# An eight-core Hyena and mixture-of-experts layer: the routing weights taken by eight compares and sums per token group instead of two maximum trees

## The chip, the cores and the metric

The kernel runs on all 8 cores of one Trainium2 chip, the same program on each, with no exchange between them. The time is device time in microseconds of the slowest core. Engines are named as in the profile: PE (TensorE), DVE (VectorE), ACT (ScalarE), POOL (GpSimd), SP (SyncE).

## The reference, cut to what matters

Input x is 4 sequences of 8192 tokens of width 1024. The layer has two halves, each with a layer norm before and behind it: a long convolution, and a mixture of 8 experts with the two best taken for each token. Only the second half is touched by the change, and in it only the weights `combine`:

```python
normed = _rmsnorm(x, norm_weight)
logits = jnp.einsum('bsd,ed->bse', normed, router_weight)      # 8 experts
probs = jax.nn.softmax(logits, axis=-1)
topk_w, topk_idx = jax.lax.top_k(probs, 2)
topk_w = topk_w / jnp.sum(topk_w, axis=-1, keepdims=True)
combine = jnp.sum(jax.nn.one_hot(topk_idx, E) * topk_w[..., None], axis=-2)
for e in range(8):
    gate, up = halves of einsum('bsd,hd->bsh', normed, gate_up_weight[e])   # 2816 each
    out_e = einsum('bsh,dh->bsd', silu(gate) * up, down_weight[e])
    moe_out = moe_out + combine[..., e, None] * out_e
```

## The kernel before

Each core takes 4096 tokens. Three stages come first, to about 1,410 us of the span: constants and the filter, input projection with short convolution, and long convolution with output projection and norms. The last one leaves `s_x1`, `s_xn2` and `s_normed` in HBM. The fourth stage, D, is the mixture, and holds all that the change touches.

Stage D runs over 4 token blocks `tb` of 1024 tokens, and in each over 8 experts `e_`. All experts are computed for all tokens. For one expert, 11 sections of weights (`guw`, two buffers, loaded by POOL's queue) are gone through; each section has four passes (two halves of the tokens by two chunks of 128 hidden columns), each of them 8 matmuls into `pg` (L1010; three PSUM buffers), 8 into `pup` (L1019; two buffers), one Silu on ACT from `pg` to `sil` (L1030) and one product on DVE, `hid` = `sil` times `pup` (L1035). PE may write a `pup` buffer again only when the product that read it is done (`pup_last`). After the sections come four quarters of the down projection (L1068, weights `dnw`), each with 8 token groups of 22 matmuls into `pd`, and DVE adds every result into `acc`, weighted by one column of `comb` (L1079 for expert 0, L1082 for the others).

The weights `comb` of block tb come from two functions. `routing_prep(tb)` loads the transposed activations `nrm` by SP's queue, lets PE compute the router logits (64 matmuls of 8 columns into `plog`, L863), and has DVE copy all 64 columns of `plog` to `cLL` (L872). `dance_tg(tb, tg)` then works on one group of 128 tokens, 8 logits each: a tree of three maxima gives the largest (L890 to L894), it is negated (L896), ACT takes the exponential of the logits (L898), the largest is masked out (L899 to L903), a second tree gives the second largest (L905 to L909), ACT takes the exponential of their difference (L913), and DVE builds the denominator, the mask of the two winners, the masked exponentials, the reciprocal and their product (L915 to L927). These are 17 DVE instructions and 2 on ACT, nearly each behind a semaphore wait on the one before; with the copy, 137 DVE instructions for one block.

Where they stand in the queues: block 0's routing comes before the first expert. Block tb+1's comes right behind expert 0's down projection of block tb, so ahead, in the order of DVE and ACT, of every Silu and every product of expert 1. For tb = 1 to 3 each expert is also followed by `e_chunk(tb - 1, e_)`, which finishes 128 tokens of the block before (L949 to L959, with a layer norm over `ffnE`). With 4 blocks there are 4 routings, and `e_chunk` stands behind the third and the fourth.

Of the kernel before, what the change touches and what calls it, by code (L numbers as in the profile page):

```python
# [7 lines left out]
F32 = mybir.dt.float32  # L8
BF16 = mybir.dt.bfloat16
AF = mybir.ActivationFunctionType  # L10
ALU = mybir.AluOpType
AX = mybir.AxisListType
# [169 lines left out]
def build_nc(debug=False, phases=("0", "AB", "C", "D"), ab_stage=5, nb=NB,  # L182
             ntb=NTB, nexp=NEXP, d_stage=4):
    nc = bass.Bass("TRN2", target_bir_lowering=False)
# [37 lines left out]
    k = K(nc)  # L222

    chb = Ch(nc, "bar")
    ch_v = Ch(nc, "v")
    ch_a = Ch(nc, "a")
    ch_p = Ch(nc, "p")
    ch_pe = Ch(nc, "pe")
# [64 lines left out]
    m1 = k.op("tensor", lambda e: e.matmul(p_h1[:, :], t_w2[:, :], t_s1[:, :], start=True, stop=True), ch_pe)  # L293
# [502 lines left out]
    if "D" in phases:  # L796
        esD = ExitStack()
# [6 lines left out]
                for p in range(2)]  # L804
        combB = [esD.enter_context(nc.sbuf_tensor(f"comb{p}", [128, (TB // 128) * 8], F32))
                 for p in range(2)]
        cLL = esD.enter_context(nc.sbuf_tensor("cLL", [128, 64], F32))
        cR = esD.enter_context(nc.sbuf_tensor("cR", [128, 8], F32))
        cE = esD.enter_context(nc.sbuf_tensor("cE", [128, 8], F32))
        cS = esD.enter_context(nc.sbuf_tensor("cS", [128, 8], F32))  # L810
        cM = esD.enter_context(nc.sbuf_tensor("cM", [128, 8], F32))
        smD = esD.enter_context(nc.sbuf_tensor("smD", [128, 16], F32))
        sil = [esD.enter_context(nc.sbuf_tensor(f"sil{i}", [128, 512], F32)) for i in range(3)]
        x1r = [esD.enter_context(nc.sbuf_tensor(f"x1r{i}", [128, 1024], BF16)) for i in range(2)]
# [9 lines left out]
        plog = esD.enter_context(nc.psum_tensor("plog", [128, 64], F32))  # L824

        NTG = TB // 128
# [6 lines left out]
        sil_last = {0: 0, 1: 0, 2: 0}  # L833
        plog_read = 0
        dance_a_prev = 0
        dance_p_prev = 0
        dance_v_prev = 0
        comb_done = {}
        uv_end = {}
        dcp_mark = {}  # L840

        ntrv = [0, 0]
        gu_end = {}

        def routing_prep(tb):
            nonlocal plog_read
            p = tb % 2
            t0p = tb * TB
            k.wait("sync", ch_pe, gu_end.get(tb - 2, 0))
            for tkb in range(2):  # L850
                for dc in range(DCN):
                    k.dma("sync", nrmB[p][tkb][:, dc * 512:(dc + 1) * 512],
                          bass.AP(s_normed, (t0p + tkb * 512) * D + dc * 128, [[D, 512], [1, 128]]),
                          ch_ntrP[p], transpose=True)
            ntrv[p] = ch_ntrP[p].n
            k.wait("tensor", ch_ntrP[p], ntrv[p])
            k.wait("tensor", ch_v, plog_read)
            for tg in range(NTG):
                tkb, tgl = tg // 4, tg % 4
                for dc in range(DCN):  # L860
                    k.op("tensor",
                         lambda e, tg=tg, tkb=tkb, tgl=tgl, dc=dc, p=p:
                         e.matmul(plog[:, tg * 8:(tg + 1) * 8],  # L863
                                  nrmB[p][tkb][:, dc * 512 + tgl * 128: dc * 512 + tgl * 128 + 128],
                                  crouter[:, dc * 8:(dc + 1) * 8],
                                  start=(dc == 0), stop=(dc == DCN - 1)),
                         ch_pe if dc == DCN - 1 else None)
            lgv = ch_pe.n
            k.wait("vector", ch_pe, lgv)
            k.wait("vector", ch_v, dance_p_prev)  # L870
            k.wait("vector", ch_a, dance_a_prev)
            dcp = k.op("vector", lambda e: e.tensor_copy(cLL[:, :], plog[:, :]), ch_v)  # L872
            plog_read = ch_v.n
            dcp_mark[tb] = ch_v.n

        def dance_tg(tb, tg):
            nonlocal dance_a_prev, dance_p_prev, dance_v_prev
            p = tb % 2
            cL = cLL[:, tg * 8:(tg + 1) * 8]
            t1 = smD[:, 1:5]  # L880
            t2 = smD[:, 5:7]
            m1 = smD[:, 0:1]
            m2 = smD[:, 7:8]
            dd = smD[:, 8:9]
            w2 = smD[:, 9:10]
            den = smD[:, 10:11]
            negm1 = smD[:, 11:12]
            k.wait("vector", ch_a, dance_a_prev)
            k.wait("vector", ch_v, dcp_mark.get(tb, 0))
            v = k.op("vector", lambda e, cL=cL: e.tensor_tensor(t1, cL[:, 0:4], cL[:, 4:8], ALU.max), ch_v)  # L890
            k.wait("vector", ch_v, v)
            v = k.op("vector", lambda e: e.tensor_tensor(t2, t1[:, 0:2], t1[:, 2:4], ALU.max), ch_v)
            k.wait("vector", ch_v, v)
            vm1 = k.op("vector", lambda e: e.tensor_tensor(m1, t2[:, 0:1], t2[:, 1:2], ALU.max), ch_v)  # L894
            k.wait("vector", ch_v, vm1)
            g4 = k.op("vector", lambda e: e.tensor_scalar(negm1, m1, -1.0, None, ALU.mult), ch_v)  # L896
            k.wait("scalar", ch_v, g4)
            s1 = k.op("scalar", lambda e, cL=cL: e.activation(cE[:, :], cL, AF.Exp, bias=negm1), ch_a)  # L898
            g = k.op("vector", lambda e, cL=cL: e.tensor_single_scalar(cR[:, :], cL, m1, ALU.is_ge), ch_v)  # L899
            k.wait("vector", ch_v, g)  # L900
            g = k.op("vector", lambda e: e.tensor_scalar(cS[:, :], cR[:, :], -1e30, None, ALU.mult), ch_v)
            k.wait("vector", ch_v, g)
            gM = k.op("vector", lambda e, cL=cL: e.tensor_tensor(cM[:, :], cL, cS[:, :], ALU.add), ch_v)  # L903
            k.wait("vector", ch_v, gM)
            v = k.op("vector", lambda e: e.tensor_tensor(t1, cM[:, 0:4], cM[:, 4:8], ALU.max), ch_v)  # L905
            k.wait("vector", ch_v, v)
            v = k.op("vector", lambda e: e.tensor_tensor(t2, t1[:, 0:2], t1[:, 2:4], ALU.max), ch_v)
            k.wait("vector", ch_v, v)
            vm2 = k.op("vector", lambda e: e.tensor_tensor(m2, t2[:, 0:1], t2[:, 1:2], ALU.max), ch_v)  # L909
            k.wait("vector", ch_v, vm2)  # L910
            g11 = k.op("vector", lambda e: e.tensor_tensor(dd, m2, m1, ALU.subtract), ch_v)
            k.wait("scalar", ch_v, g11)
            s2 = k.op("scalar", lambda e: e.activation(w2, dd, AF.Exp), ch_a)  # L913
            k.wait("vector", ch_a, s2)
            g = k.op("vector", lambda e: e.tensor_scalar(den, w2, 1.0, None, ALU.add), ch_v)  # L915
            k.wait("vector", ch_v, g)
            g = k.op("vector", lambda e: e.tensor_single_scalar(cS[:, :], cM[:, :], m2, ALU.is_ge), ch_v)
            k.wait("vector", ch_v, g)
            g = k.op("vector", lambda e: e.tensor_tensor(cR[:, :], cR[:, :], cS[:, :], ALU.add), ch_v)
            k.wait("vector", ch_v, g)  # L920
            k.wait("vector", ch_a, s1)
            gE = k.op("vector", lambda e: e.tensor_tensor(cE[:, :], cE[:, :], cR[:, :], ALU.mult), ch_v)
            k.wait("vector", ch_v, gE)
            vr = k.op("vector", lambda e: e.reciprocal(smD[:, 12:13], den), ch_v)
            k.wait("vector", ch_v, vr)
            cv = k.op("vector", lambda e, tg=tg, p=p:
                      e.tensor_single_scalar(combB[p][:, tg * 8:(tg + 1) * 8], cE[:, :],  # L927
                                             smD[:, 12:13], ALU.mult), ch_v)
            dance_a_prev = max(s1, s2)
            dance_p_prev = ch_v.n  # L930
            dance_v_prev = cv
            if tg == NTG - 1:
                comb_done[tb] = cv

        def e_chunk(tbe, tg):
            pe_ = tbe % 2
# [41 lines left out]
        gw_pending[0] = issue_gu_sections(0, 0, 0)  # L978
        gw_pending[1] = issue_gu_sections(0, 1, 0)
        routing_prep(0)  # L980
        for tg in range(NTG):
            dance_tg(0, tg)
        for tb in range(ntb):
            p = tb % 2
            nrm = nrmB[p]
            comb = combB[p]
            acc = accB[p]
            k.wait("vector", ch_v, comb_done.get(tb, 0))
            for e_ in range(nexp):
                if d_stage < 2:  # L990
                    continue
# [92 lines left out]
                        pd_last[par] = uv  # L1084
                    dn_q_end[q] = ch_pe.n
                dn_done_prev = ch_pe.n
                if e_ == nexp - 1:
                    uv_end[tb] = ch_v.n

                if d_stage >= 4:  # L1090
                    if e_ == 0 and tb + 1 < ntb:
                        routing_prep(tb + 1)
                        for tgd in range(NTG):
                            dance_tg(tb + 1, tgd)
                    if tb > 0:
                        e_chunk(tb - 1, e_)

# [106 lines left out]
```

How the kernel before makes its waits and increments, by code:

```python
    def wait(self, eng, ch, val=None):  # L51
        v = ch.n if val is None else val
        if v > 0:
            self.raw(eng, lambda e, s=ch.sem, v=v: e.wait_ge(s, v))
# [1 line left out]
    def op(self, eng, f, inc=None, k=1):  # L56
        if inc is None:
            self.raw(eng, f)
            return None
        inc.n += k
        self.raw(eng, lambda e, f=f, s=inc.sem, k=k: f(e).then_inc(s, k))
        return inc.n
# [1 line left out]
    def dma(self, eng, out, in_, inc, **kw):  # L64
        inc.n += 16
        self.raw(eng, lambda e, o=out, i=in_, s=inc.sem, kw=dict(kw):
                 e.dma_start(out=o, in_=i, **kw).then_inc(s, 16))
        return inc.n
# [1 line left out]
    def barrier(self, chb):  # L70
        chb.n += len(ENGINES)
        tgt = chb.n
        for eng in ENGINES:
            self.raw(eng, lambda e, s=chb.sem: e.sem_inc(s, 1))
            self.raw(eng, lambda e, s=chb.sem, v=tgt: e.wait_ge(s, v))
```

## Time and profile before

| what | us |
|---|---|
| median of 3 runs | 9192.27 |
| the two lowest of them | 9188.37, 9192.27 |
| the execution that was profiled | 9190.3 |
| its span on the slowest core (core 1) | 9188.8 |
| spans of the eight cores | 9170.6 to 9188.8 |

The third run took 10743.01 us, in the slower state that a program on all eight cores can fall into; it is not used. All rows below are of core 1's span. A timeline row gives start, length, engine, line, operation, output and inputs, and in square brackets how long the engine had been idle before and what ended that.

### The profile page before, as it was taken

What the parts mean: (1) busy time and instruction counts of PE and PEld (TensorE: products, weight loads), DVE (VectorE), ACT (ScalarE), POOL (GpSimd) and SP (SyncE); (2) the same over time, 40 slices, a digit from 0 to 9 for tenths busy, and PEclk for the clock granted to TensorE, in tenths of its full rate; (3) what the DMA queues carried; (4) which work ended last, traced back from release to release, by engine and by line L of the source; (5) the groups of instructions that cost most, each with busy time, mean ns of one, the idle gap of its engine ahead of it and who ended that gap; (6) DMA issues with size and microseconds to landing.
All of it is one profiled execution on the core that took longest, in us unless ns stands there. A gap on an engine that the chain in (4) does not pass through costs nothing.

```text
span 9188.8 us, 121602 instructions; the slowest of 8 cores (9170.6 to 9188.8 us)
## 1 busy us (share of the span) xinstructions
PE 8221.4 (89%) x48896; PEld 4772.1 (52%) x48896; DVE 2175.6 (24%) x3997; ACT 1440.0 (16%) x2356; POOL 1014.7 (11%) x1191
## 2 busy tenths in 40 slices
PE   4775655899999998999999998999999999999996
PEld 1322222555555555555555554555555555555554
DVE  2342442211111112222222222222222222222223
ACT  2221441111111111111111111111111111111111
POOL 1000331011111110101011110101110111111110
PEclk9887777999999999999999999999999999999998
DMA  4113435555556675565656765555555656565654
GB/s 95 61 65 78 126 117 74 66 76 76 75 75 75 76 90 67 77 80 76 81 76 81 90 81 68 75 78 76 76 77 78 81 76 81 76 81 76 80 77 85
DMA packets 1244411, 729.20 MB, mean 79 GB/s; under 512 B 103191, under 2 KB 1201047, under 8 KB 1243863
## 3 DMA queue, kind: packets, MB, share of 16 engines
q0 software_dynamic: 1110144, 584.65, 49.1%
q1 hardware_dynamic: 111064, 78.04, 3.6%
q10 hardware_dynamic: 22656, 58.73, 1.8%
q8 instruction: 403, 6.60, 0.3%
q14 instruction: 144, 1.18, 0.0%
HBM read 1198.97 MB, written 65.02 MB: 138 GB/s over the span
## 4 chain that ended last, share of the span: by engine, by line
PE 85%; DVE 6%; ACT 3%; issue 2%; POOL 1%; DMA 1%; SPq 1%; another core or an unknown queue 1%; DVEq 0%; ACTq 0%; POOLq 0%
PE pd L1068 27%; PE pup L1019 26%; PE pg L1010 25%; PE pz L453 4%; PE pcv L651 2%; PE po L687 1%; SPq L67 1%; POOL x1t L722 1%; DVE u2t L503 1%; DVE u0b L503 1%; ACT lnb L176 1%; DVE smAB L154 0%; DVE smC L154 0%; DVE ffnE L949 0%
## 5 line engine op out<-in xcount | busy, mean ns | idle before, releaser
L1019 PE MATMUL pup<-nrm,guw 128*128 128x512 bf16 x11264 | 2697.1, 383 | 221.4 <-DVE hid L1035 221.4
L1010 PE MATMUL pg<-nrm,guw 128*128 128x512 bf16 x11264 | 2676.8, 381 | 2.9 <-DMA guw<-gu_T 1.9
L1068 PE MATMUL pd<-dnw,hid 128*128 128x256 bf16 x22528 | 2466.3, 273 | 62.1 <-DVE hid L1035 60.3
L1068 PEld LDWEIGHTS pd<-dnw,hid 128*128 128x128 bf16 x22528 | 2202.7, 98 | 332.5 <-issue 77.2
L1019 PEld LDWEIGHTS pup<-nrm,guw 128*128 128x128 bf16 x11264 | 1107.5, 98 | 1576.9 <-issue 269.5
L1035 DVE TENSOR_TENSOR hid<-sil,pup 128x512 bf16<-128x512 f32 x1408 | 965.6, 687 | 3867.6 <-ACT sil L1030 3867.6
L1010 PEld LDWEIGHTS pg<-nrm,guw 128*128 128x128 bf16 x11264 | 1106.9, 98 | 1344.2 <-issue 37.0
L1030 ACT ACTIVATE sil<-pg 128x512 f32<-128x512 f32 x1408 | 838.0, 597 | 4477.1 <-PE pup L1019 4476.8
L67 POOL DMA_DIRECT2D guw<-gu_T x704 | 615.5, 881 | 5719.3 <-PE pup L1019 5713.9
L1082 DVE SCALAR_TENSOR_TENSOR acc<-pd,comb,acc 128x256 bf16<-128x256 f32 x896 | 433.4, 484 | 1749.4 <-PE pd L1068 1749.4
L651 PE MATMUL pcv<-G,ring 128*128 128x512 bf16 x768 | 186.1, 407 | 224.6 <-DVE yf L667 170.4
L453 PE MATMUL pz<-lnf,win 128*128 128x512 bf16 x1408 | 328.2, 398 | 8.5 <-DVE lnf L441 8.5
L115 ACT ACTIVATE sqE<-ffnE 128x1024 f32<-128x1024 f32 x32 | 33.8, 1057 | 1790.7 <-DVE ffnE L949 1790.7
L67 POOL DMA_DIRECT2D dnw<-dn_T x128 | 172.6, 1355 | 1169.9 <-PE pd L1068 1169.9
L651 PEld LDWEIGHTS pcv<-G,ring 128*128 128x128 bf16 x768 | 78.8, 103 | 330.7 <-issue 252.9
L453 PEld LDWEIGHTS pz<-lnf,win 128*128 128x128 bf16 x1408 | 142.2, 102 | 192.0 <-issue 41.7
L434 PE MATMUL ptr<-ident,lnb 128*128 128x128 bf16 x352 | 44.7, 301 | 197.9 <-ACT lnb L176 129.2
L486 PE MATMUL pu<-zt,cdiag 128*128 128x512 bf16 x528 | 138.8, 377 | 41.0 <-DVE u0b L503 32.5
L464 ACT ACTIVATE zt<-pz 128x512 bf16<-128x512 f32 x176 | 105.2, 598 | 329.4 <-PE pz L453 329.4
L503 DVE TENSOR_SCALAR u0b<-pu,ubias 128x512 bf16<-128x512 f32 x88 | 65.7, 747 | 339.3 <-PE pu L486 339.2
L687 PE MATMUL po<-wout,yf 128*128 128x512 bf16 x512 | 122.8, 405 | 22.6 <-DVE yf L667 22.6
L434 PEld LDWEIGHTS ptr<-ident,lnb 128*128 128x128 bf16 x352 | 31.3, 129 | 214.9 <-issue 212.3
(128 smaller groups left out, 1569.1 us busy)
## 6 DMA issues: line engine op xcount, KB each, us to landing
guw<-gu_T POOLq DMA_DIRECT2D x704, 512.0 KB, 7.8
dnw<-dn_T POOLq DMA_DIRECT2D x128, 1408.0 KB, 19.0
xa<-xs SPq DMA_DIRECT2D x11, 2048.0 KB, 8.8
xr<-xs ACTq DMA_DIRECT2D x8, 2048.0 KB, 14.3
y_out<-x2E ACTq DMA_DIRECT2D x32, 512.0 KB, 4.0
s_v<-v1b POOLq DMA_DIRECT2D x11, 1024.0 KB, 5.5
s_s<-u0b POOLq DMA_DIRECT2D x11, 1024.0 KB, 7.5
v1f<-s_v SPq DMA_DIRECT2D x8, 1024.0 KB, 8.0
```

Of the source, the lines that this page charges most:

```text
L67: e.dma_start(out=o, in_=i, **kw).then_inc(s, 16))
L453: e.matmul(pz[bank][:, :], win[:, dc * 2048 + ec * 128: dc * 2048 + ec * 128 + 128], lnf[sl][:, dc * 512:(dc + 1) * 512], start=(dc == 0), ...
L486: e.matmul(pu[bank][:, :], cdiag[:, (ec * 3 + kk) * 128:(ec * 3 + kk + 1) * 128], zt[:, ec * 516 + kk: ec * 516 + kk + 512], start=(kk == ...
L503: e.tensor_single_scalar(dstu, pu[bank][:, :], ubias[:, ec:ec + 1], ALU.add),
L651: e.matmul(pcv[bank][:, :], ring[:, (jc % 16) * 1024 + cc * 128:(jc % 16) * 1024 + cc * 128 + 128], G[:, off:off + 512], start=(i == 0), s ...
L687: e.matmul(po[bank][:, :], yf[sl][:, cc * 512 + tg * 128: cc * 512 + tg * 128 + 128], wout[:, cc * 1024 + dh * 512: cc * 1024 + (dh + 1) * ...
L1010: e.matmul(pg[par][:, :], guw[slw][:, dc * GU_SEC + hcl * 128: dc * GU_SEC + hcl * 128 + 128], nrmB[p][tkb][:, dc * 512:(dc + 1) * 512], s ...
L1019: e.matmul(pup[par][:, :], guw[slw][:, DCN * GU_SEC + dc * GU_SEC + hcl * 128: DCN * GU_SEC + dc * GU_SEC + hcl * 128 + 128], nrmB[p][tkb] ...
L1030: e.activation(sil[pr3][:, :], pg[pr3][:, :], AF.Silu), ch_a)
L1035: e.tensor_tensor(hid[:, hc * TB + tkb * 512: hc * TB + tkb * 512 + 512], sil[pr3][:, :], pup[par][:, :], ALU.mult), ch_v)
L1068: e.matmul(pd[par][:, :], hid[:, hc * TB + tg * 128: hc * TB + tg * 128 + 128], dnw[slq][:, hc * 256:(hc + 1) * 256], start=(hc == 0), sto ...
L1082: e.scalar_tensor_tensor(accv, pd[par][:, :], cc_, accv, ALU.mult, ALU.add), ch_v)
```

## The change

`dance_tg` goes, and its work moves into `routing_prep` as a loop over the 8 token groups. In each group DVE copies 8 logits from `plog` to `cL`, takes the negated maximum, and ACT takes the exponential. Then, for each of the 8 experts, DVE compares all 8 logits with that expert's logit (`is_gt`, a tensor against a per-partition scalar) and sums the result, which is that expert's rank. Ranks under 1.5 are the two winners. Their exponentials are kept, summed, and divided by the sum. These are 23 DVE instructions and 1 on ACT in a group. The place of the routing in the order of the queues is as before, and so are its loads and matmuls. The wait on `comb_done` ahead of a block's experts is dropped, and the wait on the previous exponentials is now in every group.

```diff
-        cLL = ...("cLL", [128, 64], F32)
+        cL = ...("cL", [128, 8], F32)
@@ routing_prep(tb)
-            k.wait("vector", ch_pe, lgv)
-            k.wait("vector", ch_v, dance_p_prev)
-            k.wait("vector", ch_a, dance_a_prev)
-            dcp = k.op("vector", lambda e: e.tensor_copy(cLL[:, :], plog[:, :]), ch_v)
+            for tg in range(NTG):
+                k.wait("vector", ch_pe, lgv)
+                k.wait("vector", ch_a, dance_a_prev)
+                d1 = k.op("vector", lambda e, tg=tg: e.tensor_copy(cL[:, :], plog[:, tg * 8:(tg + 1) * 8]), ch_v)
+                k.wait("vector", ch_v, d1)
+                d2 = k.op("vector", lambda e: e.reduce_max(smD[:, 0:1], cL[:, :], axis=AX.X, negate=True), ch_v)
+                k.wait("scalar", ch_v, d2)
+                d3 = k.op("scalar", lambda e: e.activation(cE[:, :], cL[:, :], AF.Exp, bias=smD[:, 0:1]), ch_a)
+                for j in range(8):
+                    dj = k.op("vector", lambda e, j=j:
+                              e.tensor_single_scalar(cR[:, :], cL[:, :], cL[:, j:j + 1], ALU.is_gt), ch_v)
+                    k.wait("vector", ch_v, dj)
+                    dj2 = k.op("vector", lambda e, j=j:
+                               e.reduce_sum(smD[:, 1 + j:2 + j], cR[:, :], axis=AX.X), ch_v)
+                    k.wait("vector", ch_v, dj2)
+                d4 = k.op("vector", lambda e:
+                          e.tensor_single_scalar(cR[:, :], smD[:, 1:9], 1.5, ALU.is_lt), ch_v)
+                k.wait("vector", ch_a, d3)
+                k.wait("vector", ch_v, d4)
+                d5 = k.op("vector", lambda e: e.tensor_tensor(cE[:, :], cE[:, :], cR[:, :], ALU.mult), ch_v)
+                k.wait("vector", ch_v, d5)
+                d6 = k.op("vector", lambda e: e.reduce_sum(smD[:, 0:1], cE[:, :], axis=AX.X), ch_v)
+                k.wait("vector", ch_v, d6)
+                d7 = k.op("vector", lambda e: e.reciprocal(smD[:, 1:2], smD[:, 0:1]), ch_v)
+                k.wait("vector", ch_v, d7)
+                k.op("vector", lambda e, tg=tg, p=p:
+                     e.tensor_single_scalar(combB[p][:, tg * 8:(tg + 1) * 8], cE[:, :],
+                                            smD[:, 1:2], ALU.mult), ch_v)
+                dance_a_prev = d3
-        def dance_tg(tb, tg):
-            ...
@@ block 0, and behind expert 0 of each block
-        for tg in range(NTG):
-            dance_tg(0, tg)
-            k.wait("vector", ch_v, comb_done.get(tb, 0))
-                        for tgd in range(NTG):
-                            dance_tg(tb + 1, tgd)
```

## Rows read from the trace of the kernel before

**Rows 1.** The page: span, busy time of PE, and the chain by engine.
```profile
span 9188.8 us, 121602 instructions; the slowest of 8 cores (9170.6 to 9188.8 us)
...
PE 8221.4 (89%) x48896; PEld 4772.1 (52%) x48896; DVE 2175.6 (24%) x3997; ACT 1440.0 (16%) x2356; POOL 1014.7 (11%) x1191
...
PE 85%; DVE 6%; ACT 3%; issue 2%; POOL 1%; DMA 1%; SPq 1%; another core or an unknown queue 1%; DVEq 0%; ACTq 0%; POOLq 0%
```

**Rows 2.** Waits of PE from 1400 us on: who, for whom, total, times, longest.
```profile
PE pup L1019 <- DVE hid L1035: 221.4, 25, 41.4
...
PE pg L1010 <- DMA guw<-gu_T: 1.9, 3, 1.0
PE pd L1068 <- DMA dnw<-dn_T: 1.8, 1, 1.8
```

**Rows 3.** Timeline of PE behind the four routings.
```profile
1484.88 3.57 PE L1019 MATMUL pup<-nrm,guw 128*128 128x512 bf16 x8 [29.71 <-DVE hid L1035]
1488.25 2.34 PE L1010 MATMUL pg<-nrm,guw 128*128 128x512 bf16 x8
...
1751.07 3.57 PE L1019 MATMUL pup<-nrm,guw 128*128 128x512 bf16 x8 [31.68 <-DVE hid L1035]
...
3643.47 3.31 PE L1019 MATMUL pup<-nrm,guw 128*128 128x512 bf16 x8 [41.42 <-DVE hid L1035]
...
5581.65 3.57 PE L1019 MATMUL pup<-nrm,guw 128*128 128x512 bf16 x8 [41.24 <-DVE hid L1035]
```

**Rows 4.** Timeline of DVE in the third routing: end of one group, start of another.
```profile
3597.34 0.23 DVE L917 TENSOR_SCALAR cS<-cM,smD 128x8 f32<-128x8 f32 x1
3597.68 0.17 DVE L919 TENSOR_TENSOR cR<-cR,cS 128x8 f32<-128x8 f32 x1
3598.01 0.17 DVE L922 TENSOR_TENSOR cE<-cE,cR 128x8 f32<-128x8 f32 x1 [0.17 <-DVE cR L919]
3598.28 0.16 DVE L924 RECIPROCAL smD<-smD 128x1 f32<-128x1 f32 x1
3598.55 0.23 DVE L927 TENSOR_SCALAR comb<-cE,smD 128x8 f32<-128x8 f32 x1
3598.73 0.16 DVE L890 TENSOR_TENSOR smD<-cLL 128x4 f32<-128x4 f32 x1
...
3599.53 0.15 DVE L896 TENSOR_SCALAR smD<-smD 128x1 f32<-128x1 f32 x1
3599.60 0.22 DVE L899 TENSOR_SCALAR cR<-cLL,smD 128x8 f32<-128x8 f32 x1
3599.93 0.17 DVE L901 TENSOR_SCALAR cS<-cR 128x8 f32<-128x8 f32 x1
3600.20 0.17 DVE L903 TENSOR_TENSOR cM<-cLL,cS 128x8 f32<-128x8 f32 x1
...
3603.49 0.16 DVE L890 TENSOR_TENSOR smD<-cLL 128x4 f32<-128x4 f32 x1
```

**Rows 5.** Timeline of DVE: first and last instructions of the first routing, first product.
```profile
1444.88 0.23 DVE L872 COPY cLL<-plog 128x64 f32<-128x64 f32 x1 [66.49 <-PE plog L863]
1445.21 0.17 DVE L890 TENSOR_TENSOR smD<-cLL 128x4 f32<-128x4 f32 x1
...
1483.62 0.23 DVE L927 TENSOR_SCALAR comb<-cE,smD 128x8 f32<-128x8 f32 x1
1484.05 1.28 DVE L1035 TENSOR_TENSOR hid<-sil,pup 128x512 bf16<-128x512 f32 x2 [0.20 <-ACT sil L1030]
```

**Rows 6.** Groups of DVE by form: names, shapes, count, busy us, mean ns, idle before.
```profile
L699 DVE TENSOR_TENSOR aot<-po,cbout 128x512 f32<-128x512 f32 x64 | 41.2, 686 | 95.3 <-PE po L687 95.3
...
L959 DVE TENSOR_TENSOR x2E<-x1r,lnE 128x1024 f32<-128x1024 bf16 x32 | 39.2, 1225 | 50.1 <-ACT lnE L133 50.1
...
L154 DVE TENSOR_REDUCE smC<-aot 128x1 f32<-128x1024 f32 x32 | 36.8, 1211 | 0.8
```

**Rows 7.** A stretch within the fourth stall: length, busy times, granted clock, DMA share, GB/s.
```profile
5540.00:5580.00 40.00, 0.42 (x2) 0.00 (x0) 22.50 (x116) 7.26 (x19) 0.00 (x0) 0.55 0.02 4
```

More of the change, by code:

```diff
@@ L806, in build_nc @@
                  for p in range(2)]
-        cLL = esD.enter_context(nc.sbuf_tensor("cLL", [128, 64], F32))
+        cL = esD.enter_context(nc.sbuf_tensor("cL", [128, 8], F32))
         cR = esD.enter_context(nc.sbuf_tensor("cR", [128, 8], F32))
         cE = esD.enter_context(nc.sbuf_tensor("cE", [128, 8], F32))
-        cS = esD.enter_context(nc.sbuf_tensor("cS", [128, 8], F32))
-        cM = esD.enter_context(nc.sbuf_tensor("cM", [128, 8], F32))
         smD = esD.enter_context(nc.sbuf_tensor("smD", [128, 16], F32))
@@ L835, in build_nc @@
         dance_a_prev = 0
[L836 to L840, printed above, removed]
         ntrv = [0, 0]
@@ L845, in routing_prep @@
         def routing_prep(tb):
-            nonlocal plog_read
+            nonlocal plog_read, dance_a_prev
             p = tb % 2
@@ L868, in routing_prep @@
             lgv = ch_pe.n
-            k.wait("vector", ch_pe, lgv)
-            k.wait("vector", ch_v, dance_p_prev)
-            k.wait("vector", ch_a, dance_a_prev)
-            dcp = k.op("vector", lambda e: e.tensor_copy(cLL[:, :], plog[:, :]), ch_v)
-            plog_read = ch_v.n
-            dcp_mark[tb] = ch_v.n
-        def dance_tg(tb, tg):
[L877 to L933, printed above, removed]
@@ L1086, in build_nc @@
                 dn_done_prev = ch_pe.n
-                if e_ == nexp - 1:
-                    uv_end[tb] = ch_v.n
                 if d_stage >= 4:
```

## The prediction

> **What bounds the kernel now.** I read the page first. PE is busy for 8221.4 of 9188.8 us and holds 85% of the chain that ended last, against 6% for DVE and 3% for ACT [rows 1]. So what PE does is the time, and a change on DVE counts only where PE stands still for it. The second view is the waits of PE from 1400 us on, which covers stage D. There PE waits for DVE's product `hid` (L1035) 25 times, 221.4 us in all, while its waits for the weight loads come to 1.9 and 1.8 us [rows 2]. The reader is to see that stage D has one kind of stall that is worth anything, and that the loads have room.
>
> The third view is PE's timeline. Four of those 25 waits stand right behind the four routings: 29.71, 31.68, 41.42 and 41.24 us, 144.1 us together [rows 3]. Their cause is the order of the queues. The routing's instructions stand on DVE ahead of the next product. PE has two `pup` buffers and three `pg` buffers, so it runs `pg`, `pup`, `pg`, `pup`, `pg` and then waits for a product that stands behind the whole routing. Nothing else is late there: DVE's first product starts 0.43 us after the routing's last instruction starts, and PE starts 0.83 us after that [rows 3, 5]. At the third and fourth routing `e_chunk` stands between the routing and the product, which makes the wait some 10 us longer but leaves it a chain in series. So every microsecond that the routing gets longer is a microsecond more of PE's stall: the cover (five groups of matmuls) is used up at 1484.88 - 29.71 = 1455.17, 10.3 us into a routing of 39 [rows 3, 5].
>
> **What one group costs now.** The routing is a chain of short instructions whose cost is the step from start to start. DVE steps on a timeline [rows 4]: a `TENSOR_TENSOR` of 8 elements followed by one wait 0.27 (L922 to L924); an immediate `TENSOR_SCALAR` of 8 elements 0.27 (L901 to L903); a `TENSOR_SCALAR` against a per-partition scalar 0.33 to 0.34 (L899 to L901, L917 to L919); an instruction of 8 followed by two waits 0.33 (L919 to L922); one followed by none 0.07 (L896 to L899); the last of a group to the first of the next 0.18 (L927 to L890). The step is thus the instruction's own length plus 0.10 to 0.11 us for the wait. A whole group takes 3603.49 - 3598.73 = 4.76 us.
>
> **What one group will cost.** By the same steps:
> - the copy of 8 logits out of PSUM. The copy of 64 takes 0.23 us [rows 5]. From `TENSOR_TENSOR` at 512 and 8 elements, (686 - 170)/504 gives 1.02 ns an element (686 ns in [rows 6], 0.17 us in [rows 4]), so the copy of 8 is 0.06 us shorter, 0.17 us, and its step 0.28. Bounds 0.26 (the shortest instruction, 0.15, plus its wait) and 0.33 (the copy of 64 as it is, L872 to L890).
> - the maximum, a reduction of 8 followed by no DVE wait: 0.07. Its exponential on ACT is wanted only after the 16 instructions that follow, so it costs nothing. The 16 instructions that cover it take 4.8 us.
> - 8 compares against a per-partition scalar, 0.335 each: 2.68.
> - 8 sums of 8. The trace has no reduction this short. At 1024 elements a reduction takes 1211 ns and a `TENSOR_TENSOR` 1225 [rows 6], so its fixed part is no bigger: 1211 - 1016 x 1.02 = 170 ns at 8 elements. Step 0.27, total 2.16. Bounds: 0.26, and 0.34 if a reduction carried the surcharge of the dearest short instruction (0.23 us long).
> - `is_lt` with two waits behind it 0.34, the product 0.27, the last sum 0.27, the reciprocal 0.27, the final product 0.17: 1.32.
>
> The sum is 0.28 + 0.07 + 2.68 + 2.16 + 1.32 = 6.51 us, against 4.76: 1.75 us more a group, 14.0 us for the eight. The old chain's trip to ACT and back (L911, L913, L915) goes, which is already in the 4.76.
>
> A rule of the Trainium skill speaks against this change: "VectorE: DVE Perf Modes", section "Rules for kernel authors", says of chained DVE operations to keep their number low and that waits don't matter, and calls a reduction on a hot path the slowest DVE operation. By number alone, 184 for 137, a routing of 39.0 us would become 52.3, 53.5 us for the four; the trace agrees in that both rates are near 0.28 us an instruction, but its 0.07 against 0.27 shows that a wait is not free. The same page's errata table gives 120 cycles plus one per element for a source in PSUM, an estimate of 133 ns for the small copy; the sum would be 1.2 us less. For 64 elements it gives 192 ns, where the trace has 225, so I keep the row.
>
> **One routing, and four.** The copy of 64 goes: -0.33 [rows 5]. The first routing lasts 1483.62 - 1444.88 = 38.74 us, where 0.33 + 7 x 4.76 + 4.58 make 38.23: 0.5 us of small pauses that no row explains. A third more instructions gives 0.2 more, at worst. One routing grows by 14.0 - 0.33 + 0.2 = 13.9 us, four by 55.5. Where no `e_chunk` follows (the first two), the product now waits 0.20 us longer than DVE needs, for a Silu that ACT starts only after its last exponential, near the end of the routing [rows 5]. After the change ACT's last exponential is 6 us before the end, so this wait goes: 0.2 to 0.3 twice, 0.5 in all. Dropping the `comb_done` wait gives nothing, since DVE has long passed it. What PE does after the stall does not change: its first eight matmuls take 3.57 us after stalls of 29.71 and 31.68 us, and 3.57 and 3.31 after 41.24 and 41.42 [rows 3]. The granted clock within the fourth stall is 0.55, near the lower of the two levels, 1.2 GHz [rows 7]. So PE's clock is already down in the stall as it is, and a stall 10 us longer has cost no more behind it.
>
> The sum is 55.5 - 0.5 = 55.0 us. Against the profiled execution: 9190.3 + 55.0 = 9245.3. That execution is 2.0 us under the median of 9192.27, so the forecast stands between 9245 and 9247, at **9246 us**, 0.6% slower.
>
> **The rivals.**
> - *Short reductions are dear.* If each of the 10 reductions of a group (9 of them followed by a wait) had the surcharge seen in the dearest short instruction, 0.07 us, that is 9 x 0.07 x 32 = 20 us more, and with the copy's upper bound 1.6 more: 9267 us. For it: no row shows one. Against it: at 1024 elements reduction and product cost the same [rows 6]. Chance 0.12.
> - *The other side: the new chain is shorter.* It would be if an instruction behind the wait on its own predecessor cost only the unwaited step of 0.07 [rows 4] in the 16 compares and sums, because they are all alike on the same small tiles. The group would cost 6.51 - 16 x 0.23 = 2.8 us instead of 4.76, the four routings 62 us less, and 1.3 less for the copies of 64: 9190.3 - 63.3, 9127 us. It decides once the mean step of the 16 falls under 0.19 us. Against it: every waited step in the old chain is 0.26 or more, whatever the tile. Chance 0.01.
> - *The loads pay it back or take more.* While PE stands longer, its weight loads land earlier. But all waits for loads in stage D are 3.7 us [rows 2], so no more than that can come back: 9242 us. Shifted against the other cores' traffic the loads could also land later; the eight cores, with the same work, differ by 18.2 us [rows 1], which I take as the size of it: up to 9264. Chance 0.07 for an effect of more than 8 us in either direction.
> - *The routing isn't on PE's path as I say,* and the stall grows by less than half: then 9192 to 9218. Against it stand four stalls that end with DVE [rows 3]. Chance 0.01.
>
> The chain as summed, 9230 to 9257 with the differences between runs and cores, keeps 0.79.
>
> **How the numbers follow.** From below, the small terms at their lower bounds give 3 + 1 us less, the loads 4, and the two lowest runs differ by 4: 9234, and a few us for shifted loads make 9230. From above, the dear reductions give 9267 and a few us for the same make 9272. Outside are the second and the fourth rival and the tails of the others, together under 0.2. About 2% is what a measurement of this kernel can tell from no change, and 2% of 9192 is 184 us. No case above reaches that: for slower the four routings would have to grow by over three times the sum. So within 2% has 0.98, and the other two 0.01 each.
>
> **What would show it right or wrong.** In the changed kernel's timeline a group (from one copy to the next) lasts 6.5 us, and a reduction of 8 is 0.16 to 0.17 us long. A routing, from its first copy to the start of its last product, lasts about 52 us. PE's four waits for `hid` behind the routings are near 43.5, 45.5, 55 and 55 us, and all 25 together near 276. The first product starts within 0.25 us of the start of the last routing instruction in the first two. PE's waits for loads stay under 5 us. Wrong would be a group far from 6.5 us, or stalls that grow by other than the routing does, or a difference that appears elsewhere in the span.

## The result

The changed kernel is slower by about what was forecast: 9244.73, 9244.75, 9247.04 and 9247.85 us, against 9188.37, 9192.27 and 9192.43 us for the kernel before, timed beside it. The ratio is 1.0059, with a 95% interval of 1.0036 to 1.0082. The forecast of 9246 us is 0.6% above the median before, as the ratio is. In the other runs of both kernels the cores of one die, or of both, had a lower granted clock (the median of all eleven timed runs is 10006.98 us, and 9804.74 for the kernel before), and the times and rows below leave such runs and dies out unless they say otherwise.

Everything in this section is read from core 1 of the profiled execution, the same core as in the rows of before. The spans and granted clocks of that execution:

```profile
core 1: 9239.9 us, clock 0.952
...
die 0 (median of its cores): 9232.8 us, clock 0.952
die 1 (median of its cores): 9974.8 us, clock 0.871
```

Core 1's span grew from 9188.8 to 9239.9 us, by 51.1. The waits of PE from 1400 us on (engine and line, for whom, total, times, longest), beside [rows 2]:

```profile
PE pup L974 <- DVE hid L990: 273.4, 25, 54.5
...
PE pg L965 <- DMA guw<-gu_T: 1.2, 3, 0.6
```

The 25 waits for `hid` went from 221.4 to 273.4 us, by 52.0. That is the whole of the longer span (what is left, 0.9 us the other way, is in small terms: the waits for weight loads, for one, fell from 3.7 to 1.2 us). PE's timeline behind the four routings, beside [rows 3]:

```profile
1500.67 3.19 PE L974 MATMUL pup<-nrm,guw 128*128 128x512 bf16 x8 [42.13 <-DVE hid L990]
...
1778.84 3.57 PE L974 MATMUL pup<-nrm,guw 128*128 128x512 bf16 x8 [44.46 <-DVE hid L990]
...
3685.74 3.57 PE L974 MATMUL pup<-nrm,guw 128*128 128x512 bf16 x8 [54.19 <-DVE hid L990]
...
5632.70 3.57 PE L974 MATMUL pup<-nrm,guw 128*128 128x512 bf16 x8 [54.47 <-DVE hid L990]
```

The four stalls grew by 12.4, 12.8, 12.8 and 13.2 us, 51.2 together. The first group of the first routing on DVE's timeline, with the first instruction of the next:

```profile
1447.70 0.17 DVE L865 COPY cL<-plog 128x8 f32<-128x8 f32 x1 [65.30 <-PE plog L856]
1447.97 0.16 DVE L867 TENSOR_REDUCE smD<-cL 128x1 f32<-128x8 f32 x1
1448.05 0.22 DVE L872 TENSOR_SCALAR cR<-cL 128x8 f32<-128x8 f32 x1
1448.38 0.16 DVE L875 TENSOR_REDUCE smD<-cR 128x1 f32<-128x8 f32 x1
1448.65 0.23 DVE L872 TENSOR_SCALAR cR<-cL 128x8 f32<-128x8 f32 x1
1448.99 0.16 DVE L875 TENSOR_REDUCE smD<-cR 128x1 f32<-128x8 f32 x1
...
1452.88 0.17 DVE L878 TENSOR_SCALAR cR<-smD 128x8 f32<-128x8 f32 x1
1453.15 0.17 DVE L881 TENSOR_TENSOR cE<-cE,cR 128x8 f32<-128x8 f32 x1
1453.42 0.16 DVE L883 TENSOR_REDUCE smD<-cE 128x1 f32<-128x8 f32 x1
...
1453.96 0.23 DVE L888 TENSOR_SCALAR comb<-cE,smD 128x8 f32<-128x8 f32 x1
1454.13 0.17 DVE L865 COPY cL<-plog 128x8 f32<-128x8 f32 x1
```

A group takes 1454.13 - 1447.70 = 6.43 us. A compare and its sum step 0.34 + 0.27 us. The short reduction, which no row of before showed, is 0.16 us long (161 ns over its 256 executions). The end of that routing:

```profile
1499.71 0.23 DVE L888 TENSOR_SCALAR comb<-cE,smD 128x8 f32<-128x8 f32 x1
1499.85 1.28 DVE L990 TENSOR_TENSOR hid<-sil,pup 128x512 bf16<-128x512 f32 x2
```

The routing lasts 52.0 us (38.7 before), and the first product no longer waits for its Silu: it starts 0.14 us after the last instruction of the routing started, 0.43 before [rows 5].

### The profile page after: what moved, and what is told of

Same layout as the page of the kernel before. It is cut to its first block, busy times and chain, and to the rows that moved or that the text cites. A ratio compares the mean times of both kernels' runs of the same rounds, so it can differ in the third digit from the quotient of the medians.

```text
span 10020.2 us, 121904 instructions; the slowest of 8 cores (9223.5 to 10020.2 us)
## 1 busy us (share of the span) xinstructions
PE 9038.6 (90%) x48896; PEld 5037.7 (50%) x48896; DVE 2217.3 (22%) x4185; ACT 1433.8 (14%) x2324; POOL 1014.7 (10%) x1191
## 4 chain that ended last, share of the span: by engine, by line
PE 86%; DVE 6%; ACT 2%; issue 2%; POOL 1%; SPq 1%; another core or an unknown queue 1%; DMA 0%; DVEq 0%; ACTq 0%; POOLq 0%
PE pd L1023 27%; PE pup L974 26%; PE pg L965 26%; PE pz L453 3%; PE pcv L651 1%; PE po L687 1%; SPq L67 1%; POOL x1t L722 1%; DVE u2t L503 1%; DVE u0b L503 1%; DVE cR L872 1%; ACT lnb L176 0%; DVE smAB L154 0%; DVE smC L154 0%
## 5 line engine op out<-in xcount | busy, mean ns | idle before, releaser
L974 PE MATMUL pup<-nrm,guw 128*128 128x512 bf16 x11264 | 2965.9, 411 | 243.8 <-DVE hid L990 243.8
L965 PE MATMUL pg<-nrm,guw 128*128 128x512 bf16 x11264 | 2950.5, 410 | 0.0
L1023 PE MATMUL pd<-dnw,hid 128*128 128x256 bf16 x22528 | 2753.2, 291 | 60.3 <-DVE hid L990 60.3
L1023 PEld LDWEIGHTS pd<-dnw,hid 128*128 128x128 bf16 x22528 | 2344.4, 104 | 476.8 <-issue 77.0
L974 PEld LDWEIGHTS pup<-nrm,guw 128*128 128x128 bf16 x11264 | 1168.8, 104 | 1801.6 <-issue 1167.6
L965 PEld LDWEIGHTS pg<-nrm,guw 128*128 128x128 bf16 x11264 | 1168.8, 104 | 1541.7 <-issue 907.6
## 6 DMA issues: line engine op xcount, KB each, us to landing
xr<-xs ACTq DMA_DIRECT2D x8, 2048.0 KB, 13.2
```

What stands on the lines that cost most here:

```text
L965: e.matmul(pg[par][:, :], guw[slw][:, dc * GU_SEC + hcl * 128: dc * GU_SEC + hcl * 128 + 128], nrmB[p][tkb][:, dc * 512:(dc + 1) * 512], s ...
L974: e.matmul(pup[par][:, :], guw[slw][:, DCN * GU_SEC + dc * GU_SEC + hcl * 128: DCN * GU_SEC + dc * GU_SEC + hcl * 128 + 128], nrmB[p][tkb] ...
L1023: e.matmul(pd[par][:, :], hid[:, hc * TB + tg * 128: hc * TB + tg * 128 + 128], dnw[slq][:, hc * 256:(hc + 1) * 256], start=(hc == 0), sto ...
```

## The experiments

The experiments were timed in four sessions, on four chips. The kernel before, timed beside them, took 9187 to 9198 us; in the session of `spread_double` and `mid` it can only be read die by die, and its dies ended at 9180 to 9194 us.

**Is every microsecond of the routing a microsecond of stall?** Two kernels change the number of compare-and-sum pairs in a group.

```diff
-                for j in range(8):
+                for j in range(4):
...
+        smz = k.op("vector", lambda e: e.memset(smD[:, :], 0.0), ch_v)
```

> The changed kernel with only 4 of the 8 compare-and-sum pairs in a group (it leaves out the ranks of experts 4 to 7, whose places in smD stay zero from one memset; so the weights are not the reference's). A pair steps 0.607 us. My theory, that every microsecond of the routing is a microsecond of PE's stall: 4 x 0.607 x 32 = 78 us less, 9168 us against 9246 for the changed kernel, below the kernel before; the 25 waits of PE for hid fall from 273 to about 196 us. Rival, that something else (loads, ACT) ends the stalls soon after: less than half of it, 9207 us or more.

Measured: 9164.20 us, against 9168; the 25 waits for `hid` are 195.3 us.

```diff
-                for j in range(8):
+                for j in list(range(8)) * 2:
```

> The changed kernel with the 8 compare-and-sum pairs of a group done twice (the second gives the same ranks). My theory: 8 x 0.607 x 32 = 155 us more, 9401 us; the 25 waits of PE for hid near 429 us; PE's clock costs nothing more behind the longer stall. Rival, that a longer stall also costs clock or upsets the loads: 9410 us or more. Rival, that part of a longer stall comes back from loads landing earlier: under 9395 us.

Measured: 9399.91 and 9402.02 us, against 9401. The waits for `hid`, first of `half`, then of `double`:

```profile
PE pup L976 <- DVE hid L992: 195.3, 25, 34.8
```
```profile
PE pup L974 <- DVE hid L990: 430.9, 25, 93.6
```

From 4 pairs through 8 to 16, the waits are 195.3, 273.4 and 430.9 us (on cores 5, 1 and 3; the cores of one run differ by about 1 us) and the times 9164, 9246 and 9401. For 128 more pairs in a kernel that is 78.1 us of wait, 0.610 each; for the next 256 it is 157.5, 0.615 each; the step on the timeline is 0.61. The line is straight from a stall of 22 us (the first one in `half`) to one of 94. Nothing to speak of comes back from the loads. A longer stall doesn't cost more clock either: read from the starts on PE's timeline, the sixteen matmuls behind each of the 25 stalls take together 49.5 us more than at full speed in the kernel before, 50.0 in the changed one and 51.0 in `double`. `half` also ends below the kernel before, so the sign of the change is this sum and nothing else.

**Is it the number of instructions or the waits between them?** In `own_buf` each compare has a buffer of its own, so that it needs no wait on the sum ahead of it. The instructions stay.

```diff
-                              e.tensor_single_scalar(cR[:, :], cL[:, :], cL[:, j:j + 1], ALU.is_gt), ch_v)
+                              e.tensor_single_scalar(cR8[:, j * 8:(j + 1) * 8], cL[:, :], cL[:, j:j + 1], ALU.is_gt), ch_v)
                     k.wait("vector", ch_v, dj)
...
-                    k.wait("vector", ch_v, dj2)
+                k.wait("vector", ch_v, dj2)
```

> The changed kernel with a cR buffer for each of the 8 compares, so that compare j+1 has no wait on sum j (each sum still waits on its compare). Same instructions, 7 waits fewer in a group. My theory, that a wait on the instruction ahead costs a step of the instruction's length plus 0.1 us, and without one the next starts 0.07 to 0.08 us after its start: 7 x (0.27 - 0.075) = 1.37 us a group, 44 us in all, 9202 us; group 5.06 us. Rival, that DVE drains between instructions whatever the waits, so that only their number counts: group 6.43 us, 9246 us.

Measured: 9195.05 and 9198.49 us, a little under the 9202 expected. On its DVE timeline:

```profile
1444.78 0.16 DVE L876 TENSOR_REDUCE smD<-cR 128x1 f32<-128x8 f32 x1
1444.86 0.22 DVE L873 TENSOR_SCALAR cR<-cL 128x8 f32<-128x8 f32 x1
1445.19 0.16 DVE L876 TENSOR_REDUCE smD<-cR 128x1 f32<-128x8 f32 x1
```

The compare starts 0.08 us after the sum ahead of it, with a wait 0.27. A group is 5.03 us (1449.13 - 1444.10). Seven waits fewer in a group are worth 1.40 us, with the same instructions, and the time is back to 5 us above that of the kernel before. In `two_rows` the 8 compares stand in a row without a wait, then the 8 sums.

```diff
                 for j in range(8):
                     dj = ... cR8[:, j * 8:(j + 1) * 8] ... is_gt
-                    k.wait("vector", ch_v, dj)
+                k.wait("vector", ch_v, dj)
+                for j in range(8):
                     dj2 = ... reduce_sum(smD[:, 1 + j:2 + j], cR8[:, j * 8:(j + 1) * 8])
                 k.wait("vector", ch_v, dj2)
```

> The changed kernel with 8 compares in a row without a wait (a buffer each), one wait, then 8 sums in a row without a wait. Same instructions. If an unwaited step is 0.075 us whatever is in front: 14 steps from 0.607/2 on average to 0.075, 3.2 us a group less, 102 us, 9144 us. If an unwaited step also depends on the length of the instruction in front (0.17 behind one of 0.23, as at the end of a group now): 2.2 us a group less, 71 us, 9175 us. Rival, that DVE drains whatever the waits: group 6.43 us, 9246 us.

Measured: 9149.66 us, between the two cases. Its timeline, where like instructions in a row are one line with their number:

```profile
1448.28 0.17 DVE L866 COPY cL<-plog 128x8 f32<-128x8 f32 x1 [65.32 <-PE plog L857]
1448.55 0.16 DVE L868 TENSOR_REDUCE smD<-cL 128x1 f32<-128x8 f32 x1
1448.62 1.16 DVE L873 TENSOR_SCALAR cR<-cL 128x8 f32<-128x8 f32 x8
1449.89 0.64 DVE L877 TENSOR_REDUCE smD<-cR 128x1 f32<-128x8 f32 x8
...
1451.88 0.17 DVE L866 COPY cL<-plog 128x8 f32<-128x8 f32 x1
```

A group is 3.60 us. The eight compares take 1.16 us, so they step (1.16 - 0.22)/7 = 0.13 us; the eight sums (0.64 - 0.16)/7 = 0.07. So an unwaited step depends on the kind of the instructions, the compare against a per-partition scalar being the slower one, and neither of my two figures held for both. The new arithmetic with 23 instructions in a group and without needless waits beats the old one with 17 by 43 us.

The rule of the Trainium skill weighed in the prediction ("VectorE: DVE Perf Modes", "Rules for kernel authors": keep the number of chained operations low, not that of the waits) doesn't hold for these short instructions: `own_buf` and `two_rows` keep the number of instructions and win 1.40 and 2.83 us a group, the first by its waits alone, the second by its waits and the order that makes them needless.

**Why was a group 6.43 us and not 6.51?** The step from `is_lt` to the product (L878 to L881) is 0.27 us, where I had put 0.34 after the old chain's L919 to L922. Both have two waits, one on DVE's own predecessor and one on ACT, but in the other order. `order_before` exchanges them in the kernel before:

```diff
-            k.wait("vector", ch_v, g)
             k.wait("vector", ch_a, s1)
+            k.wait("vector", ch_v, g)
```

> The kernel before with the two waits ahead of the masked exponentials (L922) exchanged: first the one on ACT, long fulfilled, then the one on the instruction just ahead. If the order of the waits is what makes this step 0.33 us in the kernel before and 0.27 us in the changed one, the step is 0.27 here, a group 4.69 us instead of 4.76 and the 25 waits for hid 219 instead of 221.4 us. Rival, that it is the instruction ahead (a product here, a compare there): 0.33 as before.

Measured, on core 4 of its profiled run: the step is 0.27, as the rows show (271 ns, the median of 32, against 340 in the kernel before).

```profile
1440.43 0.17 DVE L919 TENSOR_TENSOR cR<-cR,cS 128x8 f32<-128x8 f32 x1
1440.70 0.17 DVE L922 TENSOR_TENSOR cE<-cE,cR 128x8 f32<-128x8 f32 x1
```

The 25 waits are 218.6 us there and 219.3 on core 5, so 2.8 and 2.1 less. In this step, then, a wait that is long fulfilled costs nothing if it stands ahead of the one that is still open, and 0.07 us if it stands behind. This kernel has no time that could be set beside 9192 us.

**Does the routing's length matter at all where PE has slack?** The groups were taken out of their row and put behind one product each, one group in each of sections 1 to 8, of expert 0 for block 0 and of expert 1 for the others. This was done to the old groups and to the new ones (`group` below is `dance_tg` in the kernel before, and the new loop's body in the changed one).

```diff
                             sil_last[pr3] = hv
+                            if tkb == 0 and hcl == 0 and 1 <= s <= NTG:
+                                if tb == 0 and e_ == 0:
+                                    group(0, s - 1)
+                                if e_ == 1 and tb + 1 < ntb:
+                                    group(tb + 1, s - 1)
```

> The kernel before with its routing groups not in a row but one behind a product each, in sections 1 to 8 of an expert (expert 0 of block 0 for block 0, expert 1 for the later blocks). The old groups of 4.76 us then stand in DVE's queue where PE has about 3.3 us of slack and the next product is not due for 2.8 us more. Theory: no stall from them; the four stalls of 144 us shrink to the two of e_chunk, 3.7 us each; with PE's slow matmuls behind them gone too (some 2 us each), 9047 us. Rival, that the swaps of ACT's table (1.28 us twice a group) hold up the Silu and so PE: some 1 to 2 us a group, 9080 to 9110 us.

Measured: 9050.10 us.

> The changed kernel spread in the same way. Groups of 6.43 us: DVE is free for the next product 3.7 us late, PE needs its buffer 3.3 us behind the usual end, so 0.4 us of stall a group, 13 us in all. The four stalls of 196 us go but for 3.7 us twice: 9066 us. So the change costs 20 us in this place instead of 55. Rival, that the compares' 1.7 us more cost the same 55 us wherever they stand: 9100 us.

Measured: 9054.35 us, less than the 9066 expected; its profiled run took 18009.84 us, so no waits are read from it, and why no stall of 0.4 us a group shows in the time stays open. In that place the change costs 4.3 us, by one run of each, instead of 54; read die by die, the slowest cores end at 9041.7 to 9048.7 us in `spread_before` and at 9052.3 to 9055.9 in `spread_after`, 9 us apart on the average. The rest of the kernel is the same in both pairs; only where the routing stands differs. One group of `spread_before` among the products, on all engines but the weight loads:

```profile
1465.16 0.69 DVE L1033 TENSOR_TENSOR hid<-sil,pup 128x512 bf16<-128x512 f32 x1 [2.77 <-ACT sil L1028]
1465.77 0.16 DVE L890 TENSOR_TENSOR smD<-cLL 128x4 f32<-128x4 f32 x1
...
1469.33 1.89 PE L1017 MATMUL pup<-nrm,guw 128*128 128x512 bf16 x8
...
1470.34 0.23 DVE L927 TENSOR_SCALAR comb<-cE,smD 128x8 f32<-128x8 f32 x1
1470.77 0.69 DVE L1033 TENSOR_TENSOR hid<-sil,pup 128x512 bf16<-128x512 f32 x1 [0.20 <-ACT sil L1028]
1471.06 1.89 PE L1008 MATMUL pg<-nrm,guw 128*128 128x512 bf16 x8
...
1472.78 1.89 PE L1017 MATMUL pup<-nrm,guw 128*128 128x512 bf16 x8
```

The product after the group starts 2.16 us late (1470.77, where 1468.61 was due, 3.45 behind the one ahead), and PE goes on without a gap. To see where the slack ends, the new groups were spread with their pairs done twice, 11.3 us each:

> The changed kernel spread as before (one group behind a product) but with its 8 compare-and-sum pairs done twice: groups of 11.3 us instead of 6.43. If PE has a fixed slack there, the next product is late by the group less the 2.8 us it is waited for anyway, 8.5 us, of which 3.3 us are hidden: 5.2 us of stall for each of 32 groups, 166 us, and with PE's slow matmuls behind each up to 2 us more: 9220 to 9280 us. Rival, that a spread routing is hidden whatever its length: 9054 us as the spread changed kernel. Rival, that DVE's added time counts in full: 9054 + 155 = 9209 us with no cost of the clock.

Measured: 9267.81 us. PE's waits for `hid`, first of `spread_before`, then of this kernel, and PE behind the first such group:

```profile
PE pup L1017 <- DVE hid L1033: 84.8, 23, 4.0
```
```profile
PE pup L981 <- DVE hid L997: 246.9, 55, 5.6
```
```profile
1480.75 3.57 PE L981 MATMUL pup<-nrm,guw 128*128 128x512 bf16 x8 [5.05 <-DVE hid L997]
1484.12 2.86 PE L972 MATMUL pg<-nrm,guw 128*128 128x512 bf16 x8
1486.81 1.89 PE L981 MATMUL pup<-nrm,guw 128*128 128x512 bf16 x8
```

That is 162 us for 32 more waits, 5.1 each, as the slack says. The time rose by 213 us over `spread_after`, so some 50 us are left for PE's slow matmuls behind the new stalls, 1.6 us each; here 3.57 and 2.86 us instead of 1.89 make 2.65. PE's timeline says the same: the sixteen matmuls behind each stall take 98 us more than at full speed over the 55 stalls, and 45 us over the 23 of `spread_before`. This is where clock is lost, by the number of stalls and not by their length: four long ones cost no more for being twice as long (`double`), 32 short ones cost some 50 us. The shortest stalls of this run, behind the third and the fourth `routing_prep`, don't agree on where that begins. Of two that are equally long one costs clock, the other none:

```profile
3657.13 3.47 PE L981 MATMUL pup<-nrm,guw 128*128 128x512 bf16 x8 [2.30 <-DVE hid L997]
...
5606.65 1.89 PE L981 MATMUL pup<-nrm,guw 128*128 128x512 bf16 x8 [2.29 <-DVE hid L997]
```

**All groups at once.** `batch` keeps the changed kernel's arithmetic and does it for all 8 groups in one set of instructions, in the old place.

```diff
+            v = k.op("vector", lambda e: e.tensor_copy(cL[:, :], plog[:, :]), ch_v)
+            v = ... reduce_max(smD[:, 0:8], cL as 8 x 8)
+            ... tensor_tensor(cR as 8 x 8 x 8, cL repeated, cL repeated, ALU.is_gt)
+            v = ... tensor_tensor(cM, cL as 8 x 8, smD[:, 0:8] repeated, ALU.subtract)
+            s1 = ... activation(cE[:, :], cM[:, :], AF.Exp)
+            v = ... reduce_sum(cK[:, :], cR as 64 x 8)
+            ... is_lt, mult, reduce_sum to 8, reciprocal, mult, each for 64 elements
```

> The changed kernel's arithmetic for all 8 groups at once, in its place: one copy of 64, one maximum over 8 x 8, one compare of 8 x 8 x 8, one sum of 512 to 64, and so on, 10 DVE instructions and 1 on ACT for a block instead of 184 and 8. By the rows: two of 512 elements 0.8 us each with their waits, the others 0.27 to 0.34: a routing of 4.3 us instead of 52. The cover of PE is 10.3 us, so the first two stalls go, and at the other two 6.6 us are left with e_chunk. 9055 us. Rival, that compares on repeated elements (stride 0) run slower: 2 us more a routing, 9060 us, still without a stall at the first two.

Measured: no run gives one time for all eight cores. Cores 0 to 3 of one run and 4 to 7 of another end at 9036 to 9052 us, the slowest of each at 9052.3 and 9047.9, against 9055. In the profiled run even the fastest core, core 5, took 9103.7 us, so only its waits are read, not its time: its first two routings have no stall behind them, and at the third 6.14 us are left:

```profile
3597.17 3.57 PE L978 MATMUL pup<-nrm,guw 128*128 128x512 bf16 x8 [6.14 <-DVE hid L994]
```

**A version that beats both.** What is left of the waits is `e_chunk`, which stands between two experts. `mid` takes `batch`, puts its DVE part behind a product in section 1, and splits `e_chunk` in two parts (up to the norm's scale and bias, and the rest), put behind a product in sections 3 and 5 of the next expert.

```diff
+                            if tkb == 0 and hcl == 0:
+                                if s == 1 and ((tb == 0 and e_ == 0) or (e_ == 1 and tb + 1 < ntb)):
+                                    routing_dve(tb + e_)
+                                if s == 3 and pend:
+                                    e_chunk(*pend[0])
+                                if s == 5 and pend:
+                                    e_chunk2(*pend.pop(0))
-                        e_chunk(tb - 1, e_)
+                        pend.append((tb - 1, e_))
```

> What the runs point to: the routing for all 8 groups at once (4.3 us), placed behind a product in section 1, and e_chunk no longer between two experts but in two parts behind a product in sections 3 and 5 of the next expert. The 23 waits for hid that are left (85 us) go where a part fits the slack of 3.3 us behind the product's 2.8. The routing and e_chunk's second part (2.6 us of DVE, one activation) fit. In the first part ACT changes its table twice (1.28 us each) between the norm's steps, so the next product is some 4.6 us late, 1.3 us of stall 24 times, 31 us. Against 9050 us: 55 us less, and 9 us more at the end for the one chunk that is left over: 9004 us. Rival, that the first part is hidden too: 8975 us. Rival, that e_chunk's loads or its table swaps hold up more: 9050 us or more.

Measured: 8988.56 us. Its cores 0 to 3 end at 8964 to 8987 us, its cores 4 to 7 at 8942 to 8962.

> The kernel of the run mid once more, timed beside the kernel before: mid had one undisturbed run, 8988.56 us, and its waits for hid came to 37 us. If that stands, 8950 to 8990 us and a ratio of 0.974 to 0.979 to the kernel before. If the one run was a lucky one, above 9004 us.

Measured: 8954.33 us, and one die each of two more runs ends at 8954 and 8955, beside 9190.63 to 9197.51 for the kernel before in the same session. That is a ratio of 0.974, 2.6% faster than the kernel before, below the 9004 us that I had worked out. `mid` makes three changes at once (the routing in one set, its place, the split `e_chunk`), and no run separates them. The waits of PE for `hid` in the first of the two profiles:

```profile
PE pup L1024 <- DVE hid L1040: 37.3, 23, 1.9
```

They fell from 84.8 us in `spread_before` to 37.3 (31 were expected). The other 48 us of the gain over its 9050.10 us are in the matmuls behind the waits. First `spread_before` behind an `e_chunk`, then `mid` behind its first part:

```profile
4251.85 3.57 PE L1017 MATMUL pup<-nrm,guw 128*128 128x512 bf16 x8 [3.66 <-DVE hid L1033]
4255.22 3.05 PE L1008 MATMUL pg<-nrm,guw 128*128 128x512 bf16 x8
4258.10 1.89 PE L1017 MATMUL pup<-nrm,guw 128*128 128x512 bf16 x8
```
```profile
4051.83 1.89 PE L1024 MATMUL pup<-nrm,guw 128*128 128x512 bf16 x7 [1.58 <-DVE hid L1040]
4053.55 1.89 PE L1015 MATMUL pg<-nrm,guw 128*128 128x512 bf16 x8
```

After a stall of 3.66 us PE loses 2.84 us in its next sixteen matmuls, after one of 1.58 none. Over all 23 stalls, of 3.5 to 4.0 us, `spread_before` loses 45 us in this way, 1.3 to 3.0 us each. The 23 of `mid_timed`, of 1.57 to 1.86 us, lose none. My expectation had left the clock out.

## Why the prediction was right in its mechanism, and which step of it failed

- *The step that failed: the differences between runs.* The range of 9230 to 9272 us allowed for 4 us between the two lowest runs and 18.2 us between cores. The eleven timed runs lie between 9244.73 and 10854.78 us, eight of them above the range, and their median is 10006.98 us. For executions like the third run of before, 10743.01 us, the prediction had put down nothing. The kernel before spreads as widely (9188.37 to 10769.91 us, median 9804.74), so this is no effect of the change; its cause stays open. The sum and the range can be held only against the four runs in the result, 9244.73 to 9247.85 us, and all four lie within it.
- *The cause of the stalls and the rule that each microsecond counts.* Right: +52.0 us of waits for `hid` and +51.1 us of span, and a straight line from 4 to 16 pairs.
- *The steps.* The compare's 0.335 and the reduction's 0.27 (estimated from 1024 elements, 170 ns where 161 were measured) are right, the copy's 0.28 too. One term of the sum was mis-sized: `is_lt` with two waits behind it, 0.34 against 0.27. It came from a row with the waits in the other order, and it makes 0.07 x 32 = 2.2 us.
- *The pauses.* 0.5 us a routing before; now 52.0 - (7 x 6.43 + 6.26) = 0.7 in the first, so the 0.2 added was right.
- *The end of the routing.* The product's wait for the Silu went, 0.29 us in the first routing, as said.
- *The sum.* 55.0 us worked out; 51.1 on core 1, 52.0 by the waits, and 53.6 between the medians of the runs in the result (9245.9 and 9192.3). Of the 3.0 us between 55.0 and 52.0, the group of 6.43 us instead of 6.51 explains 0.08 x 32 = 2.6, most of it the mis-sized term. That 9246 meets 9245.9 so closely is in part luck: the sum was some 1 to 4 us too large, and it was set on an execution 2.0 us under the median.
- *The rivals.* Dear reductions: fell with 161 ns. A chain that steps 0.07 in spite of its waits: fell with 0.27 and 0.34. Loads: PE's waits for them went from 3.7 to 1.2 us on core 1, so 2.5 us may have come back, far from the 8 of that rival, and the line through `half` and `double` leaves no room for more. A stall that does not grow: fell.
- *The clock.* That a longer stall costs no more was argued from two lengths; `double` shows it to 93.6 us, with 51.0 us of slow matmuls behind the 25 stalls where there were 49.5. Single stalls differ more than that: behind the first routing the slow matmuls were 0.8 us less than before (3.19 and 1.89 against 3.57 and 2.34), behind the third 1.3 us more (3.57 and 2.97 against 3.31 and 1.89).

## What to carry to other kernels

Cost a chain of short DVE instructions by its steps from start to start, with the waits in them, and then ask what stands behind the chain in its engine's queue. In this kernel the same 13 us of longer routing cost 13 us each time in front of the products and 1 to 2 us when its groups stood behind a product each, where PE had 3.3 us of slack beyond the next product's due time. Before counting instructions, take out waits that a second buffer makes needless, and do the small groups in one instruction: 184 instructions in 52 us became 10 in 4 (`batch`).

## What the runs showed of the hardware

- A DVE instruction of at most 8 elements costs 0.15 to 0.23 us plus about 0.10 for a wait on its predecessor (`after`: 0.27 from a sum of 8 to the next compare, 0.33 from that compare to its sum); without the wait the next starts 0.07 us behind its start (sums, `two_rows`), 0.08 (a compare behind a sum, `own_buf`), 0.13 (compares against a per-partition scalar in a row, `two_rows`) or 0.17 (the next group's copy behind the final product, `after`).
- A fulfilled wait behind an open one costs 0.07 us, ahead of it nothing (L919 to L922: 340 ns in the kernel before, 271 in `order_before`).
- A reduction of 8 elements is 161 ns long, of 512 to 64 it is 685 ns, the same as a compare of two tensors of that size (682, `batch`).
- PE's matmuls behind a stall of 4 us are as slow as behind one of 54: 3.57 us for eight behind 3.66, 5.05 and 54.47 us of stall, at about half the speed of 1.89, and 1.89 again from the third eight on. Not every stall costs the same: the next sixteen matmuls lose 1.3 to 3.0 us, at either length (in the kernel before, 1.3 to 3.0 us behind stalls of 3.6 to 3.7 us and 1.4 to 2.1 behind 29.7 to 41.4). Behind the 23 stalls of 1.57 to 1.86 us in `mid_timed` they are at 1.89 at once. Of two stalls of 2.3 us in `spread_double` one cost 1.6 us in this way, the other nothing. In these runs, many stalls of 4 or 5 us therefore cost more than few long ones of the same sum, and those under 2 us cost only themselves.
